# Experts' gates brought to their channels by DMA instead of a selection product, with the routing parts and the turn of the gates three units sooner

## The reference, cut to what matters

```python
# 2048 tokens, 128 channels, 32 experts of 64 hidden units, one shared expert of 128
scores = sigmoid(xn @ gate_w.T)                       # 2048 x 32
choice = scores + gate_bias
group_scores = sum of the two best choices in each of 4 groups of 8
masked = choice where the group is one of the two best, else 0
w = scores at the 8 best of masked
w = 2.5 * w / (sum(w) + 1e-20)                        # the gates: 8 of 32 per token
h_e = silu(xn @ expert_gate[e].T) * (xn @ expert_up[e].T)     # 64 per expert
f = sum over e of w_e * (h_e @ expert_down[e].T) + shared expert
```

## Time and profile before

| | |
|---|---|
| median of three runs | 586.95 us (586.72, 586.95, 592.01) |
| profiled execution | 591.91 us, span from first to last instruction 590.2 |
| chain that ended last, shares by engine | PE 65%, ACT 17%, DVE 10%, issue 5%, POOL 1% |
| TensorE busy | 532.0 us (90%), 2918 products |
| VectorE busy | 475.1 us (81%) |
| ScalarE busy | 291.0 us (49%) |
| GpSimd busy | 378.9 us (64%) |
| mean granted TensorE clock | 0.947 of full speed |
| selection products (L560, pair_row) | 64, mean 395 ns |
| second multiply (L1322) | 64, mean 687 ns |

### The profile page before, as it was taken

How to read it: one execution, slowest core, us unless ns; L and a number is a source line. 1 busy time by engine, 2 the same in 40 slices (tenths; PEclk the granted TensorE clock), 3 DMA queues, 4 the chain that set the end, 5 groups by cost and what they waited for, 6 DMA issues and landing times.

```text
span 590.2 us, 8790 instructions
## 1 busy us (share of the span) xinstructions
PE 532.0 (90%) x2918; PEld 416.3 (71%) x2918; DVE 475.1 (81%) x857; ACT 291.0 (49%) x791; POOL 378.9 (64%) x326
## 2 busy tenths in 40 slices
PE   3978999999999999586999999999999999998855
PEld 3745666666666666375988888888888888887734
DVE  7676786877776666469889999999999999999785
ACT  3432242243235225314576676667667766766423
POOL 6930010021203446442999999999999999999953
PEclk9988999999999999668899999999999999999777
DMA  7440000000000000010001111110111121011002
GB/s 243 153 143 0 2 1 1 1 1 12 8 0 5 15 1 0 21 34 0 30 26 53 27 48 37 54 36 19 54 38 46 27 55 37 19 36 37 19 1 71
DMA packets 16601, 20.81 MB, mean 35 GB/s; under 512 B 2344, under 2 KB 10160, under 8 KB 16428
## 3 DMA queue, kind: packets, MB, share of 16 engines
q1 hardware_dynamic: 16556, 20.26, 11.3%
HBM read 9.76 MB, written 1.05 MB: 18 GB/s over the span
## 4 chain that ended last, share of the span: by engine, by line
PE 65%; ACT 17%; DVE 10%; issue 5%; POOL 1%; DMA 0%; ACTq 0%; POOLq 0%; DVEq 0%
PE bank L560 63%; ACT shared L1096 6%; ACT bank L1105 4%; ACT shared L1066 3%; PE bank L563 2%; ACT z_ln L1088 2%; DVE shared L1498 1%; DVE bank L1473 1%; DVE shared L1467 1%; DVE shared L1215 1%; DVE shared L1443 1%; DMA x<-in_x 0%; ACT shared L1105 0%; DVE ln_stats L1172 0%; ACT shared L981 0%
## 5 line engine op out<-in xcount | busy, mean ns | idle before, releaser
L560 PE MATMUL bank<-xnT_lo,wgu_hi 128*128 128x512 f32 x264 | 121.0, 458 | 9.2 <-ACT shared L1096 5.6
L560 PE MATMUL bank<-w,shared 128*128 128x128 f32 x1024 | 125.1, 281 | 0.3
L560 PEld LDWEIGHTS bank<-w,shared 128*128 128x128 f32 x1024 | 119.5, 195 | 6.0 <-ACT shared L1096 6.0
L560 PE MATMUL bank<-xnT_hi,wgu_lo 128*128 128x512 f32 x264 | 106.1, 402 | 0.0
L560 PE MATMUL bank<-xnT_hi,wgu_hi 128*128 128x512 f32 x264 | 105.0, 398 | 0.0
L502 POOL TENSOR_TENSOR shared<-shared 128x1024 f32<-128x1024 f32 x36 | 86.2, 2393 | 25.9 <-DVE shared L1498 25.9
L560 PE MATMUL bank<-shared 128*128 128x512 f32 (+3 forms) x280 | 88.8, 442 | 1.2 <-ACT shared L944 1.2
L966 ACT ACTIVATE shared<-bank 128x512 f32<-128x512 f32 x68 | 40.6, 597 | 96.4 <-PE bank L560 91.8
L1498 DVE TENSOR_TENSOR shared<-shared,bank 128x2048 f32<-128x2048 f32 x36 | 82.0, 2278 | 5.7 <-PE bank L560 5.7
L1473 DVE TENSOR_REDUCE bank<-shared 128x64 f32<-128x2048 f32 x36 | 82.4, 2289 | 0.3
L1096 ACT ACTIVATE shared<-bank,b 128x512 f32<-128x512 f32 x128 | 81.6, 699 | 0.0
(11 more groups left out here) (175 smaller groups left out, 806.5 us busy)
## 6 DMA issues: line engine op xcount, KB each, us to landing
w<-in_w SPq DMA_DIRECT2D x8, 256.0 KB, 3.1
shared<-in_w SPq DMA_DIRECT2D x1, 2048.0 KB, 9.3
left_tok<-state_ext SPq DMA_DIRECT2D x16, 128.0 KB
left_tok<-state_ext SPq DMA_DIRECT2D x8, 192.0 KB
shared<-in_wd SPq DMA_DIRECT2D x1, 1088.0 KB, 11.8
x<-in_x SPq DMA_DIRECT2D x4, 256.0 KB, 3.8
out<-x SPq DMA_DIRECT2D x4, 256.0 KB, 2.3
left_tok<-state_ext SPq DMA_DIRECT2D x4, 254.0 KB
```

What stands on the lines that cost most here:

```text
L560: return nc.tensor.matmul(out, lhsT, rhs, start=start, stop=stop)
```

## The change

The gates are no longer split and no longer selected by a product. VectorE writes them once, in f32 (`gates_tok`); TensorE turns 32 columns to 32 rows per tile, ScalarE copies them to `gate0T`, which now holds two batches. SyncE stores a batch's 32 x 512 gates to a scratch in DRAM and waits for that; then it loads, for every unit, two rows of them, each to 64 partitions, into `gate_rows`, a ring of three. The load of unit n waits until the second multiply of unit n - 3 is done. The second multiply takes `gate_rows` from SBUF instead of the bank GB, and waits for the two loads.

The routing parts from `route_ranks` on move: p = 8, 9, 12, 13, 14 become 7, 8, 9, 11, and the last part goes. The turn moves on TensorE from p = 15 to 12, its copy on ScalarE from p = 15 to 13, so that the store and first load of the next batch have time. SyncE's first two shifts stand now within the loads, behind those of units 36 and 52, the others after unit 63. The constants `ident_bf`, `pair_sel` and `pair_row` and their work on GpSimd go.

```diff
@@ sync
+            def rows_of_gates(n):
+                b, p = divmod(n, PAIRS)
+                if p == 0:
+                    sp.wait_ge(s("g0T_cp"), b + 1)
+                    sp.dma_start(gates_d[b], gate0T[:, b % 2]).then_inc(s("st_gates"), 16)
+                    sp.wait_ge(s("st_gates"), 16 * (b + 1))
+
+                after(sp, s("h0_done"), n - RING + 1)
+                for m in range(2):
+                    sp.dma_start(gate_rows[m * I0:(m + 1) * I0, n % RING],
+                                 gates_d[b, 2 * p + m].partition_broadcast(I0)).then_inc(s(f"ld_rows{n % RING}"), 16)
...
             sp.wait_ge(s("ld_identity"), 16 * B)
+            for n in range(B * PAIRS):
+                rows_of_gates(n)
+                if n == 2 * PAIRS + 4:
+                    shift(0)
+                elif n == 3 * PAIRS + 4:
+                    shift(1)
             for k in range(LEVELS * B):
-                shift(k)
+                if k > 1:
+                    shift(k)
@@ gpsimd
-            g.tensor_copy(ident_bf[:], ident[:]).then_inc(cdone, 1)
-            (pair_sel and pair_row: a memset, three selects, a copy)
@@ tensor
-            def gate_rows(n):
-                b, p = divmod(n, PAIRS)
-                if p == 0:
-                    pe.wait_ge(s("g0T_cp"), b + 1)
-                after(pe, s("h0_done"), n)
-                sel = pair_row[:, 2 * p:2 * p + 2].rearrange("p e i -> p (e i)")
-                mm(bank[GB][:], sel, gate0T[:, b * N:(b + 1) * N]).then_inc(s("gb_mm"), 1)
...
                 for j in range(TB):
-                    last = tr(bank[MISC if b == 0 else AT][:].bitcast(BF16)[0:3 * E0, j * P:(j + 1) * P],
-                              gate0_parts[:, b * TB + j].rearrange("p a e -> p (a e)"), ident_bf[:])
+                    last = tr(bank[MISC if b == 0 else AT][0:E0, j * P:(j + 1) * P], gates_tok[:, j])
...
-                if p == 15 and b < B - 1:
+                if p == 12 and b < B - 1:
                     gates_to_rows(b + 1)
...
                     if n >= 2:
                         gate_up(item(n), 1 + p, b)
-                    gate_rows(n)
@@ scalar
-                if p == 15 and b < B - 1:
+                if p == 13 and b < B - 1:
                     gates_out0(b + 1)
...
+                after(act, s("st_gates"), 16 * (b - 1))
+                a.copy(gate0T[:, b % 2], bank[MISC if b == 0 else AT][0:E0, :]).then_inc(s("g0T_cp"), 1)
@@ vector
             def route_gates(b):
...
-                stt(gate0_rest[:], gate0[:], ROUTED, ...).then_inc(step, 1)
-                v.tensor_copy(gate0_parts[:, tiles, 0], gate0_rest[:]).then_inc(step, 1)
-            def route_parts(b): (a subtraction, a copy, a subtraction)
+                after(dve, s("g0T_mm"), b)
+                stt(gates_tok[:], gate0[:], ROUTED, ...).then_inc(s("parts_done"), 1)
...
-                dve.wait_ge(s("gb_mm"), n + 1)
+                dve.wait_ge(s(f"ld_rows{n % RING}"), 32 * (n // RING + 1))
                 if n >= RING:
                     dve.wait_ge(s("dn_mm"), downs(n - RING))
-                tt(h0[:, n % RING], silu_gu[:, i % 2], bank[GB][:], ALU.mult).then_inc(s("h0_done"), 1)
+                tt(h0[:, n % RING], silu_gu[:, i % 2], gate_rows[:, n % RING], ALU.mult).then_inc(s("h0_done"), 1)
...
-                    elif p == 8:
+                    elif p == 7:
                         route_ranks(b + 1)
-                    elif p == 9:
+                    elif p == 8:
                         route_best(b + 1)
-                    elif p == 12:
+                    elif p == 9:
                         route_weights(b + 1)
-                    elif p == 13:
+                    elif p == 11:
                         route_gates(b + 1)
-                    elif p == 14:
-                        route_parts(b + 1)
```

More of the change, by code:

```diff
@@ L41 @@
 EXP_LN = "natural_log_exp_and_others"
-SHARED = 23500
+SHARED = 22200
 POLAR = [(8.51425808, -25.281576, 18.7673094), (4.2570752, -3.16016629, 0.586476766),
@@ L192, in build @@
         gate0 = carve(0, [P, TB, E0])
[L193 to L196, removed]
+        gates_tok = carve(0, [P, TB, E0])
+        gate_rows = sb("gate_rows", [P, RING, N])
+        gate0T = sb("gate0T", [E0, 2, N])
+        gates_d = nc.dram_tensor("gate_rows0", (B, E0, N), F32, kind="Internal").ap()
         silu_g = carve(0, [P, 2, N])
@@ L267, in build @@
             "ld_x0 ld_x1 ld_x2 ld_x3 ld_w1 ld_scan ld_gate0 ld_first ld_next ld_attn ld_l1 "
-            "ld_wg ld_wu ld_wd ld_w2_0 ld_w2_1 st_out const sel_done masks "
+            "ld_wg ld_wu ld_wd ld_w2_0 ld_w2_1 st_out const masks "
             "polar_sq_done polar_sum_mm polar_sum_cp polar_r_done polar_x0 ln_stat ln_var_done ln_pow ln_norm "
@@ L286, in build @@
         LD_ATTN, LD_L1 = 16 * 3, 16 * 5
-        IDENT_READY, CONSTS = 3, 6
+        IDENT_READY, CONSTS = 3, 5
         @block.sync
@@ L1035, in gates_out0 @@
                 act.wait_ge(s("g0T_mm"), b + 1)
-                a.copy(gate0T[:, b * N:(b + 1) * N], bank[MISC if b == 0 else AT][:].bitcast(BF16)[0:3 * E0, 0:N]).then_inc(s("g0T_cp"), 1)
+                after(act, s("st_gates"), 16 * (b - 1))
+                a.copy(gate0T[:, b % 2], bank[MISC if b == 0 else AT][0:E0, :]).then_inc(s("g0T_cp"), 1)
             silu_gate(2)
@@ L1207, in shared_hidden @@
                 tt(h_shared[:, b], silu_g[:, b % 2], bank[U[b % 2]][:], ALU.mult).then_inc(s("gu_done"), 1)
-            STEPS = 20
+            STEPS = 16
             def route_groups(b):
@@ L1279, in route_gates @@
                 dve.wait_ge(step, n + 16)
[L1280 to L1291 removed]
+                after(dve, s("g0T_mm"), b)
+                stt(gates_tok[:], gate0[:], ROUTED, wrec[:].unsqueeze(2).broadcast_to([P, TB, E0]), ALU.mult, ALU.mult).then_inc(s("parts_done"), 1)
             route_groups(0)
@@ L1402, in extras @@
                         route_masks(b + 1)
+                    elif p == 7:
+                        route_ranks(b + 1)
                     elif p == 8:
-                        route_ranks(b + 1)
+                        route_best(b + 1)
                     elif p == 9:
-                        route_best(b + 1)
-                    elif p == 12:
                         route_weights(b + 1)
-                    elif p == 13:
+                    elif p == 11:
                         route_gates(b + 1)
-                    elif p == 14:
-                        route_parts(b + 1)
                 polar_step(b, p)
```

17 lines of the change are left out of this document (1 added, 16 removed).

## The result

The changed kernel takes **593.33 us** (median of 16 runs, 591.82 to 594.24), the kernel before in the same sessions 588.49 (16 runs, 586.60 to 592.01). The ratio is 1.0081, 95% interval 1.0065 to 1.0096: slower by 0.8%, where 579.1 was forecast, and outside the range of 573.5 to 587.0. (The forecast was worked from a median of three runs, 586.95. From 588.49 the same sum gives 580.6; the change itself was forecast at -7.9 and measured at +4.8.) The profiled execution took 593.25.

The account below looks back on a forecast made before the run. The prediction took TensorE's matrix products to bound the kernel, busy 48.68 of batch 1's 48.98 us. Terms -14.0 - 0.5 + 0.5 + 1.8 + 3.3 + 1.0 = -7.9 us took 586.95 to 579.1; range 573.5 to 587.

Parts of the forecast that it names:

- Steps 1 and 2: Unit loop: selection product gone, 61 x 0.23 = -14.0 us; TensorE's wait for the second multiply gone, -0.5 us.
- M: Experiments' rival: the second multiply, with two SBUF inputs, is held up by GpSimd; the prediction's C, chance 0.17.
- Step 3: The turn: four bf16 turns per batch become four f32 turns, three batches at +0.15, +0.5 us, between 0 and 1.8.
- Step 4: VectorE: four instructions a batch go, routing parts move to units 7 to 11, lateness is covered: 0 us.
- step 6: Units 37 and 53: loads stand behind the shifts in SyncE's queue, +3.3 us, and the clock drops, +1.0 us.
- Step 5: Start: round trip of gates through DRAM replaces existing waits, +0.1; slow clock after TensorE's idling, +1.7; together +1.8 us.
- Step 7: GpSimd and batch borders: constants taken out save nothing, store and load fit into the units left: 0 us.
- B: Rival: the shift doesn't block the loads, so 3.3 + 1.0 us aren't paid: 574.8 us; chance 0.18.
- C: Rival: second multiply, reading two SBUF inputs, is held by GpSimd; if a third reaches TensorE, 4 us: 583.1; chance 0.17.
- D: Rival: the loads set the pace through the ring of three rows; at 9 us landing, 612 us; chance 0.09.
- E: Rival: nothing moves, TensorE's saved work is filled by waits for ScalarE and VectorE: 587 us; chance 0.14.

Follow-up runs that it names:

- e5: The kernel before without the 64 selection products and the wait for them, nothing in their place (experts' gates left out of the computation): 573.18 us, ratio 0.9753.
- e9: e6 with the turn and copy of batch 0's gates ahead of the first unit's gate and up products and silu: 572.33 us, ratio 0.9703.
- e2: The kernel before with only the level-0 shifts' 127 partitions moved in pieces of 112 and 15: 588.96 us, ratio 1.0016.
- e4: The kernel before, selection product kept, with only the routing parts, turn and copy moved to their new places: 588.65 us, ratio 1.0000.
- e1: The changed kernel with the level-0 shifts' 127 partitions moved in pieces of 112 and 15: 577.86 us, ratio 0.9834.
- e3: The changed kernel with the shifts of batches 0 and 1 left whole but issued behind the last load: 579.01 us, ratio 0.9848.
- e7: The changed kernel with whole shifts issued behind the loads of units 33 and 49 in place of 36 and 52: 591.33 us, ratio 1.0059.
- e8: The changed kernel with whole shifts on SyncE's queue, but the loads of gate rows issued by ScalarE, one unit ahead: 584.92 us, ratio 0.9953.
- e11: e9 with the first multiply's product in SBUF, as in the changed kernel, so the second multiply reads two SBUF tiles: 574.03 us, ratio 0.9733.
- e6: e1 with the first multiply's product in the bank GB, so the second multiply reads one bank and one SBUF tile: 577.05 us, ratio 0.9818.

## Why the prediction was wrong, by its steps

**Steps 1 and 2 (product and its wait, -14.5): right, the exact figure in part by luck.** e5 measures -14.5, of which 12.4 lie in units 3 to 63 and 1.8 before, where the steps had all of it in the loop. The changed design gets there too: without the shift's waits and with M away, e9's loop is 14.4 us shorter than e2's. Batch 1 takes 45.46 us where 45.3 was forecast, and TensorE is busy 44.96 of it.

**Step 3 (turn, +0.5): right.** Four f32 turns are busy 0.60 us as forecast. From their start to TensorE's next product it is 0.43 us (78.88 to 79.31), for the old bf16 turns 0.19 (88.64 to 88.83): so three batches cost 0.7 more.

**Step 4 (VectorE, 0): right.** e4 gives no difference. One slip: the step quotes step 6 with 4.1 us of lateness of which 2.0 arrive; step 6 itself has 4.8, so the slack it reckons with is 2.8 us, not 2.1.

**Step 5 (start, +1.8): mis-sized.** The mechanism was right: TensorE stood 4.40 us where 4.5 was said, and the clock fell behind it, for 2.8 us of matrix time where 1.7 was taken. The rows landed at 47.6, sooner than the 49.9 forecast: the copy of the turned gates ended at 42.33 instead of 44.1, and the store took 1.64 instead of 2.3; the two loads took 3.57 as against 0.4 + 3.1. What failed is the thing that the start was compared with. I took unit 3's gate product at 51.91 from a profile whose start ran at a clock of 0.70, and called that a price "paid already". e2, and e4 with it, show 1.00 in that stretch and unit 3's second multiply 3.5 and 3.1 us sooner. Against e2's start the new one is 3.8 us later there, where 1.8 was forecast (e2's execution is itself 1.9 under its median, so between 1.9 and 3.8). The page of the profile had the hint: the profiled execution was 5 us above the median, and I wrote that the loop's rows don't depend on which. The loop's didn't (180.56 and 180.59); the start's did.

**Step 6 (loads behind the shift, +3.3, and clock, +1.0): the step that failed.** Its mechanism is what happened, and e1 and e3 show it by taking it away. Its size was 4.3 (3.3 of standing, 1.0 of clock); after against e1 the loop pays 183.12 - 167.41 = **15.7 us**. Of these 8.5 lie between units 36 and 52, behind the first shift, 6.6 between 52 and 63, behind the second, and 0.6 before unit 36, where the starts still differ. So the term measured **15.1 us**, not 4.3. For the first shift, with H the end of unit 33's multiply (138.13 in the trace after; all times below count from it):

- The row landed at 17.0 instead of 15.4, the multiply ended at 17.8 instead of 16.1. The 1.5 us to land were enough: it was 1.2 from the shift's completion write at 153.98. But the shift's transfer took 14.7 us, from 139.29 to 153.98, where 12.7 was taken from the kernel before. Why it is longer with loads around it stays open.
- TensorE could go on at 19.2 instead of 18.2.
- TensorE ran dry at 13.7 (151.87), where I had it busy until 16.2. The step followed the late multiply to unit 40's gate product, and passed over the polar product of unit 38's extras. That one stands before it in TensorE's order, with unit 39's gate and up products behind it, and waits for L1351, which stands behind the late multiply. This is the largest piece of the error in the standstill: 2.5 us.
- Together 2.0 (forecast) + 1.0 + 2.5 = 5.5, the 5.43 of the row.
- The clock: 3.0 us behind that gap and 1.7 behind the second (4.71 us of standing, where 1.3 was forecast), where +1.0 was taken for both. My upper bound was 1.7 for each, from a stretch of 0.70; behind the first gap the clock was at 0.50 from the restart on and for 5.7 us.

5.43 + 3.0 = 8.4, against the 8.5 measured; 4.71 + 1.7 = 6.4, against 6.6. Of the error of 10.8, 6.8 is standing still, 3.7 the clock, and 0.3 isn't placed. e7 shows that the polar product isn't all of it: without it in the way two longer waits still cost 12.2 us (179.60 - 167.41). In a loop where TensorE is busy 99% of the time, nothing gives a stop back.

The Trainium skill, "DMA: Bandwidth & Descriptors", section "Why a DMA increments its semaphore by 16 and not by 1", gives a DMA the largest number of engines up to 16 that divides its slowest dimension, here the partitions: one for 127, and by the same rule sixteen for 112 and fifteen for 15. By that rule e1 should run the shift at many times the rate, and the runs agree: 18 to 25 GB/s and waits of 6.31 and 6.13 us with 127, a shift of under 3 us and no wait with 112 and 15. The Trainium skill, in the same page, section "Queues, rings and completion order", has each engine go round between the queues for which it has work. e8 agrees, in that loads from another queue land sooner beside the shift (7.0 us at most instead of 10.3).

**Step 7 (borders, 0): right.** No wait for a store or first load at a border.

**Rivals.** B (no blocking) is false, since the loads waited. C (multiply held by GpSimd) exists and is small: 0.6 to 1.2 us of the loop, with 4 reckoned. D (loads set the pace) is false: the median landing is 2.9 us, and no unit other than 0, 37 and 53 waited. E (nothing moves) is false by batch 1. The result ended on the slower side by none of the mechanisms that I had there, but by the forecast's own one at three and a half times its size.

How the result is made up, in medians: -14.5 (e5) + 4.7 for the round trip, the turn and the multiply (e1 over e5) + 15.5 for the two shifts (after over e1) = +5.7. These three meet the difference of the changed kernel and e5's own kernel before (593.33 - 587.64) by construction, so the sum proves nothing. Directly measured it is 593.33 - 588.49 = +4.8; the rest is what medians of different sessions differ by.

## What to carry to other kernels

When a new transfer joins a queue, list what else stands in that queue, and look at the slowest transfer in it by its shape: a DMA over 127 partitions ran at a DMA share of 0.06 to 0.08, about one engine of sixteen, and in two pieces of 112 and 15 it was out of the way. Price a late semaphore by walking the list of the engine that sets the pace, instruction by instruction, up to the first that depends on anything behind the late one, and add the clock after a gap of some us as a term of its own size. And before a row of the start serves as a reference, compare its clock and the run's time with the median: here the row was 3.5 us later than in another execution of the same program.

## What the runs showed of the hardware that was not expected

- The issue of the small DMA behind the 127-partition one is blocked on SyncE for 4.02 us in the kernel before and for 5.79 in e8. In the kernel after it takes 1.47 us and the load behind it 3.23; at the second shift it takes 4.19. In e3, where whole shifts follow each other, it takes up to 9.76. In e1, behind 112 and 15 partitions, it takes 0.56.
- What a gap of TensorE cost in clock, from the restart on. Nothing behind 1.51 and 1.52 us (e8) and 1.62 (e9); 1.6 to 1.7 us of matrix time behind 2.08 (e11), 3.04 and 3.24 (e7), 4.34 (e6), 4.45 (e1) and 4.71 (after, second shift), so that in these the price hardly depends on the gap's length. In all six the clock was still 1.00 until the last half us of the gap. Where it had fallen to 0.50 sooner, it cost more: 2.5 behind 4.90 (e3), 2.8 behind 4.40 (after, start), 3.0 behind 5.43 (after, first shift). The gap's length alone doesn't decide: at the start of the kernel before, 1.83 us cost nothing and 1.77 cost 2.0, and e1 and the kernel after have nearly the same gap at the start (4.45 and 4.40) and pay 1.7 and 2.8. What does decide is open.
- A load of two rows of 2 KB from DRAM, each to 64 partitions (128 KB per issue), lands in 2.9 us, the store of 64 KB in 1.6.
